# Attention's first group takes its rows by token halves, later stages' semaphores are credited in the first stage, and the output is stored in parts

## The chip, the cores and the metric

One Trainium2 chip, one of its cores. Five engines work side by side, each with an instruction stream of its own: TensorE (PE, with its weight loads shown as PEld), VectorE (DVE), ScalarE (ACT), GpSimd (POOL) and SyncE (SP), which here only issues transfers. They wait for each other through semaphores. The metric is the time of one execution on the device in microseconds; lower is better.

## The reference

Six blocks follow each other on x of 2 sequences x 1024 tokens x 256 channels, each behind a layer norm and added to x:

```
x = x + 0.5 * moe(norm(x))          # 16 experts, top 2, 256 -> 512 -> 256, silu
x = x + attention(norm(x))          # 16 heads of 16; scores of later keys are 0, not left out
x = x + 0.5 * moe(norm(x))
x = x + 0.5 * lora_ffn(norm(x))     # base linear + 8 low-rank experts, top 2
x = x + latent_attention(norm(x))   # 16 heads, rotary part, low-rank keys and queries
x = x + 0.5 * lora_ffn(norm(x))
```

## The kernel before

The kernel is written engine by engine. A stage is a `Block` in which each engine has its own program, and at the end of a block all engines meet in a barrier. x stays on the chip in the tile `X` (128 partitions x 16 token tiles x 256). The stages are `moe` (twice, with a short `load_stage` ahead of the first), `att`, `lora` 0, `mla`, `lora` 1 and a `store_stage`. Order within a stage is the order in which the code is written.

**Semaphores.** Nearly every semaphore of the kernel is counted from 1 (`Sem.base` is 1), and SP adds that 1 at the start of the stage in which the semaphore first occurs (`credit`, L113 to L117). The engines of a stage wait for the last one credited, as in `act.wait_ge(s_x.handle, s_x.at(0))`, before they do anything. Each credit is one instruction of SP on L116.

**Norms.** `norm_sd_act` (L131) waits for the means and variances `MV`, then takes the square root on ScalarE. ScalarE needs a function table for that (ACT_TABLE_LOAD). The moe, mla and second lora stages use it; attention and the first lora stage take four tiles at a time (`part_sd_act`, L143).

**Sums of the experts.** After a moe stage the two expert outputs of each token lie in DRAM (`rows_out`). The next stage loads them in four groups of four tiles (`ExpertSums.load`, tiles `Y1` and `Y2`, 512 KB a transfer) and DVE adds them to x two tiles at a time (`ExpertSums.add`, L219 to L234). `Y2` holds eight tiles, so groups 2 and 3 wait until groups 0 and 1 are added.

**Attention.** Heads are worked off in eight groups G of four. For each, `projections` makes 512 columns (a token half) of queries and keys, ACT and DVE split them into a high part `SH` and a low part `SL`, and SP places their rows in `QT` and `KT` by 12 transfers of 128 KB (L765) after both halves are made. `rough_scores` then makes score pieces of 128 to 512 keys, of which DVE takes the maxima (L1171, L1173); the first 16 pieces or so (`NPC0`) belong to the first 512 tokens, and need only keys of that half. `QT` and `KT` are first filled by ACT (L1099, L1100), for both buffers of the ring. In the front of the stage (before the loop over G) DVE adds the sums (`summed(0)` to `summed(3)`), normalizes tiles 0 to 7, makes the low parts and then runs `maxima(0, ...)`. PE transposes tiles 0 to 7, projects the two halves of group 0, multiplies the values of tiles 0 to 7 (`values`, L857) and then starts `rough_scores`.

**Lora.** For 16 tiles, PE transposes the rows (L1343), makes `mids` (L1335), then `base` (L1353) for tiles 0 to 3, into PSUM banks 4 to 7. While DVE works out the routing of tiles 8 to 15 PE waits; then, tile by tile, PE turns the gated mids (L1359), adds their product (L1390) to the base in its bank, DVE updates X (`updated`, L1509), and PE makes the base three tiles ahead as soon as the bank is free. The first lora stage also prepares weights for mla (`queries_into_keys`, `values_into_output`), which use banks 0 to 3 and are copied out by ACT.

**Store.** `store_stage` is a block of its own with one transfer of 2 MB (L2291).

## Time and profile before

| | |
|---|---|
| median of 3 runs | 2308.17 us (2306.41 to 2308.9) |
| time of the profiled execution | 2314.1 us |
| its span in the trace | 2312.4 us |
| PE busy | 2027.0 us (88%) |
| DVE busy | 1306.3 us (56%) |
| ACT busy | 787.8 us (34%) |
| POOL busy | 872.7 us (38%) |
| mean granted clock of PE | 0.928 |

The span is that of the trace, from the first to the last record. Roughly, moe 0 runs from 0 to 285 us, attention to 749, moe 1 to 1020, lora 0 to 1112, mla to 2253, lora 1 to 2304, and the store to the end. An engine's share of the whole says little about the places where the stages meet, since there most engines are idle together.

### The profile page before, as it was taken

To read this page: it belongs to the slowest core of one execution; us is meant where nothing else is said; L and a number is where in the kernel's file an instruction comes from. 1 tells how busy PE (TensorE), PEld (TensorE's weight loads), DVE (VectorE), ACT (ScalarE), POOL (GpSimd) and SP (SyncE) were. 2 spreads that over 40 slices of the span, in tenths; PEclk is the share of its full clock that TensorE was granted. 3 is DMA by queue.
4 is the path that set the end of the run, shared out by engine and by line. 5 is a ranking of instruction groups with operands and counts; after the bars stand their busy time and mean duration, and the time that the engine had idled before them with its cause. 6 is when DMAs were issued, how large, how long until landed. Compare 5 with 4: busy or idle time off the path is not lost. (4 is left out here: it accounts for less than half of the span.)

```text
span 2312.4 us, 29499 instructions
## 1 busy us (share of the span) xinstructions
PE 2027.0 (88%) x8740; PEld 1262.9 (55%) x8741; DVE 1306.3 (56%) x2992; ACT 787.8 (34%) x1297; POOL 872.7 (38%) x690
## 2 busy tenths in 40 slices
PE   5899859898988799965679999999899999999986
PEld 5566535455544666644545555555565555555455
DVE  6322265777785722236456667666656666666525
ACT  1122244555554122223214333334413333333312
POOL 0344301231112044431025555565325555555622
PEclk9999958999999599987679999999999999999998
DMA  9121242232220711232132211222022222222001
GB/s 370 46 63 61 53 118 28 28 44 39 28 28 7 332 55 64 60 103 105 43 70 55 52 46 42 54 54 55 18 65 55 55 50 55 54 54 51 9 2 47
DMA packets 59656, 151.40 MB, mean 65 GB/s; under 512 B 12768, under 2 KB 18096, under 8 KB 57264
## 3 DMA queue, kind: packets, MB, share of 16 engines
q1 hardware_dynamic: 49008, 120.43, 20.1%
q0 software_dynamic: 9408, 25.70, 3.8%
q10 hardware_dynamic: 1152, 4.19, 0.4%
q8 instruction: 43, 0.70, 0.1%
q14 instruction: 45, 0.37, 0.1%
HBM read 69.47 MB, written 18.87 MB: 38 GB/s over the span
## 5 line engine op out<-in xcount | busy, mean ns | idle before, releaser
L1723 POOL TENSOR_TENSOR mla_PS<-mla_PS,mla_PT 128x1024 f32<-128x1024 f32 x192 | 457.8, 2384 | 227.9 <-ACT mla_PT L2002 225.3
L2145 DVE TENSOR_REDUCE mla_MXP<-PS 128x1 f32<-128x512 f32 x512 | 343.4, 689 | 245.7 <-PE PS L1802 241.2
L2002 ACT ACTIVATE mla_PT<-PS 128x1024 f32<-128x1024 f32 x256 | 262.3, 1025 | 406.5 <-PE PS L1821 404.0
L1830 PE MATMUL PS<-mla_PT,mla_CN 128*64 128x512 f32 x1024 | 276.0, 618 | 0.1
L486 DVE COPY moe_HT<-PS 128x512 f32<-128x512 f32 x96 | 66.4, 692 | 320.0 <-PE PS L603 313.9
L1802 PE MATMUL PS<-mla_KH,mla_QH 113*128 113x512 f32 x512 | 216.7, 459 | 32.5 <-DMA mla_KL<-mla_SL 21.3
L618 POOL DMA_INDIRECT moe_XS<-rows_in,moe_GI x100 | 97.4, 974 | 317.1 <-PE PS L586 178.5
L1821 PE MATMUL PS<-mla_QH,mla_KH 113*128 113x512 f32 x512 | 211.9, 414 | 1.0 <-ACT mla_QH L1989 1.0
L1821 PE MATMUL PS<-mla_QL,mla_KH 113*128 113x512 f32 x512 | 202.8, 396 | 0.0
L1821 PE MATMUL PS<-mla_QH,mla_KL 113*128 113x512 f32 x512 | 201.6, 394 | 0.0
L1802 PEld LDWEIGHTS PS<-mla_KH,mla_QH 113*128 113x128 f32 x512 | 90.9, 193 | 194.5 <-DVE mla_MXP L2145 123.5
L1072 ACT ACTIVATE att_PT<-PS 128x1024 f32<-128x1024 f32 (+1 forms) x192 | 152.0, 811 | 94.4 <-PE PS L912 92.9
L597 PE MATMUL PS<-W,moe_ST 128*128 x384 | 177.6, 606 | 2.7 <-DVE moe_ST L481 2.7
L1723 POOL TENSOR_TENSOR mla_PS<-mla_PT 128x1024 f32<-128x1024 f32 x32 | 76.3, 2383 | 264.6 <-ACT mla_PT L2002 264.6
L611 PE MATMUL PS<-W,moe_HT 128*128 x768 | 173.7, 379 | 0.0
L891 PE MATMUL PS<-att_KT,att_QT 128*128 128x512 f32 (+3 forms) x384 | 146.1, 426 | 27.5 <-DVE att_MX L1173 10.1
L1171 DVE CUSTOM_DVE_ANT_0 PS<-PS,att_SEEN 128x128 f32<-128x128 f32 (+3 forms) x256 | 122.8, 508 | 55.6 <-PE PS L891 53.2
L611 PEld LDWEIGHTS PS<-W,moe_HT 128*128 128x128 f32 x768 | 142.3, 190 | 17.3
L791 POOL TENSOR_SCALAR_AFFINE_SELECT att_PT<-att_PT 128x256 f32<-128x256 f32 x128 | 52.0, 407 | 252.9 <-ACT att_PT L1072 252.8
L2157 DVE RECIPROCAL PS<-PS 128x128 f32<-128x128 f32 x128 | 108.7, 918 | 59.9 <-PE PS L1837 59.9
L1821 PEld LDWEIGHTS PS<-mla_QH,mla_KH 113*128 113x128 f32 x512 | 97.1, 190 | 80.6 <-issue 34.3
L891 PEld LDWEIGHTS PS<-att_KT,att_QT 128*128 128x128 f32 x384 | 75.6, 212 | 105.6 <-DVE att_MX L1173 38.5
(291 smaller groups left out, 3243.8 us busy)
## 6 DMA issues: line engine op xcount, KB each, us to landing
W<-in_W_dram SPq DMA_DIRECT2D x16, 2048.0 KB, 27.6
sums_Y<-rows_out SPq DMA_DIRECT2D x16, 512.0 KB, 4.9
mla_QH<-mla_SH SPq DMA_DIRECT2D x64, 128.0 KB, 2.4
mla_KH<-mla_SH SPq DMA_DIRECT2D x64, 128.0 KB, 2.4
mla_QL<-mla_SL SPq DMA_DIRECT2D x64, 128.0 KB, 2.4
mla_KL<-mla_SL SPq DMA_DIRECT2D x64, 128.0 KB, 2.4
mla_KH<-mla_SH SPq DMA_DIRECT2D x64, 96.0 KB, 2.4
mla_KL<-mla_SL SPq DMA_DIRECT2D x64, 96.0 KB, 2.4
```

What stands on the lines that cost most here:

```text
L597: ins = pe.matmul(bank(2 + u)[:, :], ST[:, u, k, :], g.W1[:, experts[u], k, :], start=(k == 0), stop=(k == KD - 1))
L611: ins = pe.matmul(bank(6 + u)[:, 0:D], HT[:, u, k, :], W2[:, experts[u], k, :], start=(k == 0), stop=(k == KF - 1))
L891: ins = pe.matmul(out[:, m, :], QT[:, H % 2, h, i * P:(i + 1) * P], KT[:, H % 2, h // 2, k0:k0 + w], start=(m == 0), stop=(m == len(hs) - 1))
L1072: act.activation(PT[:, kk % 2, 2 * pair:2 * pair + 2, c0:HB], st_banks(s)[:, :, c0:HB], ACT.Exp, scale=SEQ ** -0.5).then_inc(s_p.handle, 1)
L1171: ins = dve.tensor_tensor_reduce(part, part, seen, 1.0, LEAST, ALU.mult, ALU.max, MX[:, q, c, h, t:t + 1])
L1723: pool.tensor_tensor(PS[:, :], PT[:, slot(0), :] if k == 1 else PS[:, :], PT[:, slot(k), :], ALU.add).then_inc(s_ps.handle, 1)
L1802: pe.matmul(bank(piece_bank(n))[:, :], QH[USED, buf, h, tile * P:(tile + 1) * P], KH[USED, buf, h, c * HB:(c + 1) * HB], start=True, stop= ...
L1821: ins = pe.matmul(bank(st_bank(s, h))[:, :], kk[USED, buf, h, ks], qq[USED, buf, h, qs], start=(n == 0), stop=(n == 2))
L1830: ins = pe.matmul(bank(6)[h * DKVL:(h + 1) * DKVL, :], CN[:, b, k, 0:DKVL], PT[:, slot(k), h * HB:(h + 1) * HB], start=(k == 0), stop=(k = ...
L2002: act.activation(PT[:, slot(k), :], banks(st_bank(s, 0), 2)[:, :], ACT.Exp, scale=MLA_SCALE).then_inc(s_p.handle, 1)
L2145: dve.tensor_reduce(MXP[:, n // NPC, c, h, t:t + 1], bank(piece_bank(n))[:, :], AX_X, ALU.max).then_inc(s_mx.handle, 1)
L2157: dve.reciprocal(bank(A)[:, cols], bank(A)[:, cols]).then_inc(s_rc.handle, 1)
```

## The change

Seven edits, in the order of the program. (1) The square root's table is loaded ahead of the wait in `norm_sd_act`, in attention and in the first lora stage. (2) The first moe stage's SP program credits, after its own semaphores, all those of the later stages (`LATER`, a tuple of 100 or so names). (3) Group 0 of the sums is loaded in two halves of two tiles with a semaphore each; in attention `Y2` now lies in the tile `PT`, holds 16 tiles, and groups 2 and 3 no longer wait. (4) Attention's group 0 places its rows by token halves, in 24 transfers of 64 KB, the first 12 with a semaphore of their own; `rough_scores` of the first block waits for those alone. DVE makes the first low part ahead of `summed(2)`, PE multiplies the values of tiles 0 and 1 between the halves, and ACT's fills of the second buffer stand behind the row copies. (5) The lora stages keep six bases in PSUM in place of four. (6) PE's wait for the lora weights stands ahead of the first `mids` and no longer ahead of the first transposes. (7) The second lora stage stores the output in four parts of 512 KB, each after four tiles are updated, and `store_stage` is gone.

```diff
 def norm_sd_act(act, g, s_mv, s_sd):
+    g.nc.scalar.preload_act_table(ACT.Sqrt)
     act.wait_ge(s_mv.handle, s_mv.at(NT))
...
+            if n == 0:
+                for half in range(2):
+                    tiles = slice(2 * half, 2 * half + 2)
+                    sp.dma_start(self.Y1[:, tiles, :], rows(0)[:, tiles, :]).then_inc(self.s_in[half].handle, 16)
+                    sp.dma_start(self.Y2[:, tiles, :], rows(1)[:, tiles, :]).then_inc(self.s_in[half].handle, 16)
+            else:
+                sp.dma_start(self.Y1[:, tiles, :], rows(0)[:, tiles, :]).then_inc(self.s_in[n + 1].handle, 16)
+                sp.dma_start(self.Y2[:, ring, :], rows(1)[:, tiles, :]).then_inc(self.s_in[n + 1].handle, 16)
...
                 g.credit(sp)
                 if rep:
                     expert_weights(g, dram, rep)(sp)
+                else:
+                    for name in LATER:
+                        g.sem(name)
+                    g.credit(sp)
...
-        expert = g.sums.buffers(ctx)
+        expert = g.sums.buffers(ctx, PT[:, :, :, :].rearrange("p u h (n d) -> p (u h n) d", d=D))
...
-                sp.wait_ge(s_afill.handle, s_afill.at(4))
                 for G in range(NG):
+                    if G < 2:
+                        sp.wait_ge(s_afill.handle, s_afill.at(2 * (G + 1)))
...
+                    for half in range(2 if G == 0 else 1):
+                        tok = slice(half * HB, (half + 1) * HB) if G == 0 else slice(0, SEQ)
+                        s_placed = s_first if G == 0 and half == 0 else s_rows
...
+                            sp.wait_ge(s_made.handle, s_made.at(half + 1 if G == 0 else 2 * (G + 1)))
...
-                        if n == 0:
+                        if H == 0 and n == 0:
+                            pe.wait_ge(s_first.handle, s_first.at(NROW))
+                        elif n == (NPC0 if H == 0 else 0):
                             pe.wait_ge(s_rows.handle, s_rows.at(NROW * (H + 1)))
...
                     projections(0, half, bank(4 + half))
-                for t in range(TB):
-                    if t >= 2:
-                        pe.wait_ge(s_vc.handle, s_vc.at(t - 1))
+                    if half == 0:
+                        for t in range(2):
+                            values(t, bank(2 + t))
+                for t in range(2, TB):
+                    pe.wait_ge(s_vc.handle, s_vc.at(t - 1))
                     values(t, bank(2 + t % 2))
...
+                low(0, 0, bank(4))
                 summed(2)
-                low(0, 0, bank(4))
                 low(0, 1, bank(5))
...
+    BASE = (4, 5, 6, 7, 2, 3)
+    NB = len(BASE)
...
+                if out is not None:
+                    s_out = g.sem("x_stored")
+                    rows = out.rearrange("b (t p) d -> p (b t) d", p=P)
+                    for n in range(NB4):
+                        tiles = slice(n * NT // NB4, (n + 1) * NT // NB4)
+                        sp.wait_ge(s_x.handle, s_x.at((n + 1) * NT // NB4))
+                        sp.dma_start(rows[:, tiles, :], g.X[:, tiles, :]).then_inc(s_out.handle, 16)
+                    sp.wait_ge(s_out.handle, s_out.at(16 * NB4))
...
-                pe.wait_ge(s_w.handle, s_w.at(64))
-
                 def mids_of(t):
+                    if t == 0:
+                        pe.wait_ge(s_w.handle, s_w.at(64))
...
+                pe.wait_ge(s_xtc.handle, s_xtc.at(NT))
                 if ahead:
-                    pe.wait_ge(s_xtc.handle, s_xtc.at(NT))
                     queries_into_keys()
                     values_into_output(0)
                     values_into_output(1)
-                    pe.wait_ge(ahead.s_abc.handle, ahead.s_abc.at(2))
+                    pe.wait_ge(ahead.s_abc.handle, ahead.s_abc.at(6))
+                else:
+                    pe.wait_ge(s_mid.handle, s_mid.at(NT))
+                for t in range(NR, NB):
+                    base(t)
...
-            lora_stage(nc, g, dram, 1)
-        store_stage(nc, g, out)
+            lora_stage(nc, g, dram, 1, out=out)
```

How the instructions stand, at the places of which the prediction speaks. First ScalarE at the start of attention, before (`att_QT`, `att_KT`: the fills; `att_XT`: transposed rows; `att_SH`: high parts; `att_VV`: values; SD: the root):

```order
L1099 ACTIVATE att_QT<-C 128x4096 [waits att_x_updated]
L1100 ACTIVATE att_KT<-C 128x2048
L1099 ACTIVATE att_QT<-C 128x4096
L1100 ACTIVATE att_KT<-C 128x2048
L147 ACT_TABLE_LOAD
L147 ACTIVATE SD<-MV,C 128x4 [waits norm_stats]
L1035 COPY att_XT<-PS 128x2x128 [waits att_xnT_in_psum] x4
L1049 CAST att_SH<-PS 128x512 [waits att_qk_in_psum]
L147 ACTIVATE SD<-MV,C 128x4 [waits norm_stats]
```

And of the change:

```order
L1147 ACT_TABLE_LOAD [waits att_x_updated]
L1142 ACTIVATE att_QT<-C 128x4096
L1145 ACTIVATE att_KT<-C 128x2048
L166 ACTIVATE SD<-MV,C 128x4 [waits norm_stats]
L1076 COPY att_XT<-PS 128x2x128 [waits att_xnT_in_psum] x4
L1142 ACTIVATE att_QT<-C 128x4096
L1092 CAST att_SH<-PS 128x512 [waits att_qk_in_psum]
L166 ACTIVATE SD<-MV,C 128x4 [waits norm_stats]
L1080 COPY att_VV<-PS 128x16x16 [waits att_values_in_psum] x2
```

The table and one pair of fills stand ahead of the first root; the second pair has moved behind the first copies, and two copies of values stand behind the second root.

Second SP at the same place, from the weights on, before (`sums_Y`: expert sums; 12 transfers of L765, of which the first two stand here):

```order
L753 DMA att_Wo<-in_Wo_dram 128x512
L216 DMA sums_Y<-rows_out 128x1024 [waits moe_second_added,moe_expert_out_stored]
L217 DMA sums_Y<-rows_out 128x1024
L216 DMA sums_Y<-rows_out 128x1024 [waits moe_second_added]
L217 DMA sums_Y<-rows_out 128x1024
L765 DMA att_QT<-att_SH 16x2x1024 [waits att_high_parts,att_filled_by_act]
L765 DMA att_KT<-att_SH 16x2x1024
```

And of the change:

```order
L786 DMA att_Wo<-in_Wo_dram 128x512
L244 DMA sums_Y<-rows_out 128x1024 [waits moe_expert_out_stored]
L245 DMA att_PT<-rows_out 128x1024
L244 DMA sums_Y<-rows_out 128x1024
L245 DMA att_PT<-rows_out 128x1024
L802 DMA att_QT<-att_SH 16x2x512 [waits att_high_parts,att_filled_by_act]
L802 DMA att_KT<-att_SH 16x2x512
```

The groups behind the weights have lost their wait for DVE, and the row transfers carry 512 tokens each (12 of them for each half).

Third TensorE in the second lora stage, behind the first bases, before:

```order
L1353 MATMUL PS<-lora_Wbase,lora_XT 128x256 x8
L1359 MATMUL PS<-C,lora_GM 128x128 [waits lora_gated] x2
L1390 MATMUL PS<-lora_B,lora_MT 128x256 [waits lora_midsT_copied]
L1359 MATMUL PS<-C,lora_GM 128x128 [waits lora_midsT_copied,lora_gated]
L1390 MATMUL PS<-lora_B,lora_MT 128x256 [waits lora_midsT_copied]
L1353 MATMUL PS<-lora_Wbase,lora_XT 128x256 [waits lora_x_updated]
```

And of the change:

```order
L1416 MATMUL PS<-lora_Wbase,lora_XT 128x256 x8
L1416 MATMUL PS<-lora_Wbase,lora_XT 128x256 [waits lora_mids_copied,lora_xnT_copied]
L1416 MATMUL PS<-lora_Wbase,lora_XT 128x256 x3
L1422 MATMUL PS<-C,lora_GM 128x128 [waits lora_gated] x2
L1457 MATMUL PS<-lora_B,lora_MT 128x256 [waits lora_midsT_copied]
L1422 MATMUL PS<-C,lora_GM 128x128 [waits lora_midsT_copied,lora_gated]
L1457 MATMUL PS<-lora_B,lora_MT 128x256 [waits lora_midsT_copied]
L1416 MATMUL PS<-lora_Wbase,lora_XT 128x256 [waits lora_x_updated]
```

Two bases (four rows) have moved ahead of the first turn of gated mids; the loop that follows makes 10 bases where it made 12.

## Rows read from the trace of the kernel before

**Rows 1.** Page, parts 1 and 2: busy time, and PE's granted clock in tenths by 40 slices.

```profile
PE 2027.0 (88%) x8740; PEld 1262.9 (55%) x8741; DVE 1306.3 (56%) x2992; ACT 787.8 (34%) x1297; POOL 872.7 (38%) x690
...
PEclk9999958999999599987679999999999999999998
```

**Rows 2.** Instructions of L116 in attention, lora 0 and mla: ns, first and last start.

```profile
L116 SPq EVENT_SEMAPHORE  x37: 17/17/17, 285.4 to 288.0; - x37
...
L116 SPq EVENT_SEMAPHORE  x26: 17/17/17, 1019.8 to 1021.3; - x26
...
L116 SPq EVENT_SEMAPHORE  x38: 17/17/17, 1111.9 to 1114.0; - x38
```

**Rows 3.** Timeline of attention's front: start, duration, operation [idle before <-releaser].

```profile
293.43 0.88 DVE L225 SCALAR_TENSOR_TENSOR X<-sums_Y,GH,X 128x256 f32<-128x256 f32 x2 [4.54 <-DMA sums_Y<-rows_out]
...
298.74 1.28 ACT L147 ACT_TABLE_LOAD   x1
...
301.13 1.09 PE L851 MATMUL PS<-C,att_XNS 128*128 128x128 f32 x4 [19.16 <-DVE att_XNS L159]
...
307.76 0.58 ACT L1049 CAST att_SH<-PS 128x512 fp32r<-128x512 f32 x1 [3.87 <-PE PS L876]
...
310.80 0.88 DVE L225 SCALAR_TENSOR_TENSOR X<-sums_Y,GH,X 128x256 f32<-128x256 f32 x2
...
315.55 7.07 PE L857 MATMUL PS<-att_Wv,att_XT 128*128 128x256 f32 x32
...
323.25 0.43 DVE L153 RECIPROCAL RS<-SD 128x4 f32<-128x4 f32 x2 [1.30 <-ACT SD L147]
...
331.94 0.30 DVE L1171 CUSTOM_DVE_ANT_0 PS<-PS,att_SEEN 128x128 f32<-128x128 f32 x1 [8.25 <-PE PS L891]
...
341.20 0.17 DVE L1183 TENSOR_SCALAR att_MB<-att_MX 128x16 fp32r<-128x16 f32 x1
```

**Rows 4.** Line L765, 310 to 332 us: one form of its four, and issue to landing.

```profile
L765 SPq DMA_DIRECT2D att_QT<-att_SL x2: 591/592/592, 322.2 to 323.5; - x2
...
DMA to landing us min/median/max: 3.5/5.7/7.4
```

**Rows 5.** Timeline: last weight load of attention, and line L753 from issue to landing.

```profile
291.08 0.43 SPq L753 DMA_DIRECT2D att_Wo<-in_Wo_dram  x1
...
DMA to landing us min/median/max: 8.0/8.0/8.0
```

**Rows 6.** Timeline: the root's table in moe 0 (first two) and mla.

```profile
15.33 1.28 ACT L134 ACT_TABLE_LOAD   x1 [15.33 <-DVE MV L128]
16.62 0.31 ACT L134 ACTIVATE SD<-MV,C 128x16 f32<-128x16 f32 x1
...
1115.35 1.28 ACT L134 ACT_TABLE_LOAD   x1 [5.76 <-DVE MV L128]
```

**Rows 7.** Timeline: start of lora 0, first addition.

```profile
1026.72 0.88 DVE L225 SCALAR_TENSOR_TENSOR X<-sums_Y,GH,X 128x256 f32<-128x256 f32 x2 [12.81 <-DMA sums_Y<-rows_out]
```

**Rows 8.** Timeline: start of lora 1.

```profile
2258.22 1.12 PE L1343 MATMUL PS<-C,lora_XN 128*128 128x128 f32 x4 [6.29 <-DMA lora_biases<-in_biases_dram]
...
2259.37 1.27 PE L1335 MATMUL PS<-lora_Wlora,lora_XT 128*128 128x136 f32 x4
```

**Rows 9.** Timeline: updates of X in the last stage (tiles 11, 13, then 14 and 15).

```profile
2299.73 0.42 DVE L1509 SCALAR_TENSOR_TENSOR X<-PS,X 128x256 f32<-128x256 f32 x1 [0.78 <-PE PS L1390]
...
2302.54 0.42 DVE L1509 SCALAR_TENSOR_TENSOR X<-PS,X 128x256 f32<-128x256 f32 x1 [0.98 <-PE PS L1390]
...
2303.16 0.97 DVE L1509 SCALAR_TENSOR_TENSOR X<-PS,X 128x256 f32<-128x256 f32 x2 [0.20 <-PE PS L1390]
```

**Rows 10.** The store: timeline, transfers (KB each, us to landing), and L216, a 512 KB load.

```profile
2304.49 0.40 SPq L2291 DMA_DIRECT2D out_dram<-X  x1
...
out_dram<-X SPq DMA_DIRECT2D x1, 2048.0 KB, 7.5
...
DMA to landing us min/median/max: 3.9/4.1/6.3
```

More of the change, by code:

```diff
@@ L197, in __init__, with buffers @@
         self.s_yd = S("expert_out_stored", 16 * NTILE, pool_dma=True)
-        self.s_in = [S(f"sums_loaded{n}", 32) for n in range(self.NG)]
+        self.s_in = [S(f"sums_loaded{n}", 32) for n in range(self.NG + 1)]
         self.s_first, self.s_second, self.s_stats = S("first_added", NT), S("second_added", NT), S("row_stats", NT)
         self.rep = rep
-    def buffers(self, ctx):
-        self.Y1, self.Y2 = (self.g.sb(ctx, f"sums{self.rep}_{n}", [P, tiles, D]) for n, tiles in (("Y1", NT), ("Y2", NT // 2)))
+    def buffers(self, ctx, second=None):
+        name = f"sums{self.rep}_Y"
+        self.Y1 = self.g.sb(ctx, name + "1", [P, NT, D])
+        self.Y2 = self.g.sb(ctx, name + "2", [P, NT // 2, D]) if second is None else second
+        self.y2_tiles = NT // 2 if second is None else NT
         return self
@@ L1256, in _, with lora_stage @@
                     updated(TB + i, bank(i % 2))
-def lora_stage(nc, g, dram, rep, ahead=None):
+def lora_stage(nc, g, dram, rep, ahead=None, out=None):
     S = lambda name, each: g.sem("lora_" + name, each, rep)
@@ L1389, in _ @@
                     pe.wait_ge(s_mtc.handle, s_mtc.at(t + 1))
-                    pe.matmul(bank(4 + t % NR)[:, 0:D], MT[:, t % NR, :], BL[:, :], start=False, stop=True).then_inc(s_lo.handle, 1)
-                    if t and t + NR - 1 < NT:
-                        base(t + NR - 1)
+                    pe.matmul(bank(BASE[t % NB])[:, 0:D], MT[:, t % NR, :], BL[:, :], start=False, stop=True).then_inc(s_lo.handle, 1)
+                    if t and t + NB - 1 < NT:
+                        base(t + NB - 1)
             @block.scalar
             def _(act):
-                if not sums:
+                if sums:
+                    nc.scalar.preload_act_table(ACT.Sqrt)
+                else:
                     norm_sd_act(act, g, s_mv, s_sd)
@@ L2282, in _ @@
                         updated(b, i)
-def store_stage(nc, g, out):
-    s_out = g.sem("x_moved")
-    with nc.Block() as block:
-        @block.sync
-        def _(sp):
-            g.credit(sp)
-            sp.dma_start(out.rearrange("b (t p) d -> p (b t) d", p=P), g.X[:, :, :]).then_inc(s_out.handle, 16)
-            sp.wait_ge(s_out.handle, s_out.at(16))
 def macaron_program(nc, dram, out, stages="mamlLl"):
```

64 lines of the change are left out of this document (44 added, 20 removed).

## The prediction

> **What bounds the kernel now.** I read the page first: TensorE is busy 88% of the span [rows 1], so where it is dense only less work for it would help, and this change takes none away. What the change touches are the seams between stages. There the question is which wait ends last, and I read that from the timeline around each seam, with idle time and its releaser. Four kinds of waste show.
>
> First, SP's credits. In attention 37 of them run from 285.4 to 288.0 us, in lora 0 26 from 1019.8 to 1021.3, in mla 38 from 1111.9 to 1114.0 [rows 2]; no engine does work of the stage before the last one. That is 2.6, 1.5 and 2.1 us, or 0.07 us each. Second, in moe 0 ScalarE's table load starts only when the norm's inputs are there (15.33), and the root follows at 16.62 [rows 6]: 1.28 us on a chain on which everything else of the stage waits. It is the same in moe 1 and mla. Third, attention's front. DVE gets the first sums at 293.43; it starts the maxima at 331.94 after 8.25 us of idling, because the rows of the whole first group had to land; before that it was never long idle, from 310.80 to the last reciprocal at 323.25 to 323.68 [rows 3]. So behind the row transfers DVE is next in line. Fourth, the end: the last update ends at 2303.16 + 0.97 = 2304.13, and the store of 2 MB is issued at 2304.49 and lands 7.5 us later [rows 9, 10].
>
> **The change part by part.**
>
> *Root's table.* Loaded ahead of the wait, it runs in idle time (ScalarE sits idle 15.33 us before it in moe 0 and 5.76 in mla). That gives 1.3 us each in moe 0, moe 1 and mla: 3.9. If the cover were gone it would cost the 1.28 it costs now. The root starts 0.01 us after the load [rows 6], so I count the load alone. The Trainium skill (ScalarE: Activation LUTs, What ACT_TABLE_LOAD costs) gives about 2.66 us for a switch of tables, 1283 ns for the load and about 1380 for a drain. The trace agrees on the load and shows no drain here; by the page the three places would give 8.0 in place of 3.9.
>
> *Credits.* They move to SP in moe 0, behind the semaphores on which that stage's start depends, and SP has nothing else to do there. About 103 x 0.07 = 7 us of SP, hidden behind 270 us of moe 0. One semaphore more stands ahead (the halves of group 0): +0.07. Gain 2.6 in attention (counted below), 1.5 in lora 0, 2.1 in mla.
>
> *First sums by halves.* A 512 KB transfer takes about 4.1 us to land [rows 10], the first addition waits for two of them, and I take the second to add some 1.2 us (2 MB of the store land in 7.5 us, against 4.1 for a quarter of it: 3.4 / 3 = 1.1). With half the bytes it starts about 1.2 us earlier, in attention and in lora 0, where the first addition at 1026.72 is waited for after 12.81 us of idling [rows 7]. Between nothing and 2 us. What follows in lora 0 is DVE's own work, so it carries over. Groups 2 and 3 without waits in attention: DVE never waited for them, nothing.
>
> *Attention's front.* The first addition comes at 293.43 - 2.6 - 1.2 = 289.6. Four tiles are done 5 us later, 294.6, and ScalarE has then been free since 292.2 (285.4, the table 1.28, a pair of fills 5.5); before, its two pairs of fills and the table load ended at 300.02 [rows 3]. That would be 5.4 earlier, but PE also waits for the last weight, which landed at 291.08 + 8.0 = 299.1 [rows 5]. It has the same bytes ahead of it and starts 2.6 earlier: 296.5. So PE's first transposes move from 301.13 to 296.5, by 4.6. The high part of half 0 moves from 307.76 to 303.1 likewise. Then PE does the values of tiles 0 and 1: 7.07 us for eight tiles [rows 3] is 0.9 for one at the high clock (1.8 at the low one, at which this place ran), 1.8 to 3.5 us where it had idled 1.6. So the second half of the transposes comes up to 1.8 later than it could, and DVE begins low part and sums at 310.80 - 4.6 + 1.8 = 308.0, against 306.2 without that. DVE's chain of low parts, sums and reciprocals took 323.68 - 310.80 = 12.9 us, and it had to wait 1.3 us in it for ScalarE, which stood in values copies. Some 0.9 of that goes, since two copies are out of the way: it ends at 320.0. Are the rows there? SP issues half 0 from 303.7: eight high transfers at 0.6 us [rows 4], four low ones behind DVE's low part at 308.7, issued by 311.2, landed by 314.7 (3.5) or 318.6 (7.4). PE's values end at about 318. So DVE no longer waits and the maxima start at 320.0 in place of 331.94: 11.9 us. With the high clock at TensorE in this stretch (it projects and multiplies values without a break for 7 us) the 1.8 falls away: 13.7. I take 12.5, between the two and nearer the low clock, at which the rows ran.
>
> The second half's rows must be there when the first block's maxima end. These took 341.20 - 331.94 = 9.3 us, so 329.3. High part 1 at about 313; SP issues 12 transfers at 0.6 us each, to 320.5, and they land 3.5 to 7.4 later, 324 to 328. That is covered, by 1 to 5 us; every us beyond would count fully. ScalarE's second pair of fills is behind the copies and hidden in the projections; if it is not, it costs up to 3.6.
>
> *Six banks.* In the loop of both lora stages a tile with a base takes 1.41 us (2299.73 to 2302.54 is two), and without one about 0.6 (2302.54 to 2303.16) [rows 9]. Two bases move to where PE waits for the routing: 2 x 0.8 = 1.6 us in each stage. In lora 0 they stand behind ScalarE's copies of the absorbed weights, still in DVE's routing time.
>
> *Lora 1's start.* PE's first transposes at 2258.22 were released by the weights' transfer; they now go ahead, and the first mids take their place, which came at 2259.37 [rows 8]: 1.15. The root's table is hidden here by the same transfer, so I count nothing for it.
>
> *Store.* The last part is 512 KB and is issued some 0.1 us after the last update, without a barrier. Loads of that size took 3.9 to 6.3 us, median 4.1 [rows 10]. Against 2304.49 + 7.5 - 2304.13 = 7.9 it ends 3.9 earlier, or 1.5 by the slow end. The earlier parts have 1.4 us a tile to run in and are gone.
>
> **Sum.** Moe 0 1.2, attention 12.5, moe 1 1.3, lora 0 1.5 + 1.2 + 1.6 = 4.3, mla 2.1 + 1.3 = 3.4, lora 1 1.1 + 1.6 + 3.9 = 6.6: 29.3 us. The profiled execution took 2314.1, so 2284.8; the median of the runs is 5.9 lower, 2308.2, so **2279 us**, 1.3% less.
>
> **The rivals.**
>
> *A: attention's front gives little.* The row transfers stay last: 24 that each occupied their queue as a whole one did. The 12 were issued 0.6 us apart, and issue to landing grew from 3.5 to 7.4 us [rows 4], so the queue took 0.6 + 3.9 / 12 = 0.93 us for each. Halves at the same price land by 303.7 + 12 x 0.93 + 2.9 = 317.8 for half 0, and about 329 for half 1 (behind half 0 in the queue). That just meets the 329.3. Together with a high part that comes late by 3.6 (the fills) the front gives 7 in place of 12.5: 2284. The Trainium skill (DMA: Bandwidth & Descriptors, Bandwidth) speaks against this edit: it asks for transfers of 1 MiB or more and calls those under 64 KB descriptor-dominated, with 0.95 us for 64 KB. By the page a half takes 11.4 us of queue; half 1 would land at about 326, and the time would not change.
>
> *B: TensorE's clock helps.* In the profile it was at 0.5 to 0.9 in two places, attention's front and the start of moe 1 [rows 1]. The change fills idle time of PE between the halves and in both lora stages; if the clock stays at 2.4 GHz through the rough scores, the pieces and later values run faster by up to 5 us: 2273.
>
> *C: the page's price for tables.* If the root's table really held up 2.66 us each, the gain is 4 more: 2275. Against it speaks the 0.01 us between load and root.
>
> *D: no change.* The seams could be bound by something else that comes at a fixed time, a transfer above all. For lora 1's start this is so and counted; elsewhere the releasers are the credits, DVE and ScalarE. Then within 0.2% of before: 2306.
>
> *E: slower.* The granted clock of TensorE. The main loops of attention and mla are PE's, and mostly at full clock [rows 1]. A us at half clock there costs about half a us. If moving the stages made the clock low for 60 us more than before, the 29 are gone, and beyond that it is slower; at 80 us the time is 2319. The slices show some 4 to 6 of 40 with any low share outside the fronts, so this would be several times what there is. Nothing in the change makes PE idle in those loops.
>
> **How the numbers follow.** Forecast (22 to 36 us gained) 0.82, A 0.09, B in its full size (over 36) 0.03, C 0.02, D 0.01, E 0.03. The bounds of the unknown costs are: attention 11 to 17 (low or high clock), store 1.5 to 4.4, halves of sums 0 to 4 in both, banks 0 to 3.5. Not all fall on one side; 2269 to 2289 holds the forecast's body and part of A, and leaves 2 in 10 out. Within 0.2% (4.6 us), about what a measurement of this kernel can tell from no change: 0.02. Faster by more: 0.95; slower by more: 0.03.
>
> **What the new profile would show.** Attention's first DVE addition about 4 us after the last engine of moe 0; ScalarE's root ahead of any second fill; maxima starting right behind the reciprocals, with no idle time released by PE's rough scores; that idle time would prove A. Credits of L116 nearly all in the first 30 us. Lora's updates 0.6 us apart for the last five tiles. The last store landing about 4 us after the last update. The prediction is wrong if DVE idles again for rows, if PE waits for the weights beyond 297, or if PEclk is lower in mla.

## The result and the profile after

The changed kernel takes 2278.89 us (median of four runs, 2278.29 to 2280.76), the kernel before 2308.18 (2306.41 to 2308.9): a ratio of 0.9876, with a 95% interval of 0.9858 to 0.9893. The forecast was 2279. The traced execution took 2279.0 us with a span of 2277.3. Its page, parts 1 and 2, answers to [rows 1]:

```profile
PE 2015.8 (89%) x8740; PEld 1256.3 (55%) x8741; DVE 1306.4 (57%) x2992; ACT 788.2 (35%) x1297; POOL 872.5 (38%) x690
...
PEclk9999969999999599987679999999999999999999
```

TensorE does the same 8740 matmuls, its share of a shorter span is higher, and of the clock's digits the 5 and 8 of attention's front have become 6 and 9 and the last 8 a 9.

Attention's front, timeline of the changed kernel; it answers to [rows 3]:

```profile
287.30 0.88 DVE L254 SCALAR_TENSOR_TENSOR X<-sums_Y,GH,X 128x256 f32<-128x256 f32 x2 [3.00 <-DMA att_PT<-rows_out]
...
296.41 1.09 PE L888 MATMUL PS<-C,att_XNS 128*128 128x128 f32 x4 [16.48 <-DMA att_Wo<-in_Wo_dram]
...
302.58 1.89 PE L894 MATMUL PS<-att_Wv,att_XT 128*128 128x256 f32 x8
302.78 0.59 ACT L1092 CAST att_SH<-PS 128x512 fp32r<-128x512 f32 x1
...
304.37 0.73 PE L888 MATMUL PS<-C,att_XNS 128*128 128x128 f32 x4
...
306.58 1.98 PE L913 MATMUL PS<-att_XT,att_Wqk 128*128 128x512 f32 x4 [0.46 <-ACT att_XT L1076]
...
313.39 0.75 PE L930 MATMUL PS<-att_KT,att_QT 128*128 128x128 f32 x4
...
317.24 0.30 DVE L1224 CUSTOM_DVE_ANT_0 PS<-PS,att_SEEN 128x128 f32<-128x128 f32 x1
...
326.51 0.18 DVE L1236 TENSOR_SCALAR att_MB<-att_MX 128x16 fp32r<-128x16 f32 x1
```

TensorE's first transposes are released by the last weight at 296.41 (296.5 was forecast). The maxima start at 317.24 with no bracket behind them: the 8.25 us of idling are gone, and DVE goes on where its last reciprocal ends. The first rough scores (L930) start at 313.39, so the rows of the first half were there 3.8 us before DVE was. The row transfers, all 24, by line (one form of four) and their landing; this answers to [rows 4]:

```profile
L802 SPq DMA_DIRECT2D att_QT<-att_SL x4: 583/592/593, 309.3 to 318.5; - x4
...
DMA to landing us min/median/max: 2.2/2.2/2.6
```

The credits, and the last two updates, against [rows 2] and [rows 9]:

```profile
L134 SPq EVENT_SEMAPHORE  x154: 17/17/17, 0.8 to 20.4; - x154
```

```profile
2271.19 0.42 DVE L1578 SCALAR_TENSOR_TENSOR X<-PS,X 128x256 f32<-128x256 f32 x1 [0.79 <-PE PS L1457]
...
2271.81 0.97 DVE L1578 SCALAR_TENSOR_TENSOR X<-PS,X 128x256 f32<-128x256 f32 x2
2272.97 0.97 DVE L1578 SCALAR_TENSOR_TENSOR X<-PS,X 128x256 f32<-128x256 f32 x2 [0.20 <-PE PS L1457]
```

All credits lie in the first 20.4 us, and the last five updates are 0.6 us apart. The span ends 4.33 us after 2272.97; before it was 2312.4 - 2303.16 = 9.24.

**Where the time went, stage by stage.** I traced both kernels a second time. The table gives the length of each stretch in both traces of each, from starts read in the timelines; its ends are the last scatter of moe 0 on POOL, attention's first maxima, attention's last row statistics, the last copy of moe 1 on DVE, the last statistics of lora 0, mla's reciprocal, mla's last statistics, the start of the last two updates, and the end of the span. The gain is the difference of the two means.

| stretch | before (2 traces) | changed (2 traces) | gain | forecast |
|---|---|---|---|---|
| moe 0 | 282.66, 282.90 | 280.62, 281.50 | 1.7 | 1.2 |
| attention to the first maxima | 49.28, 49.41 | 36.62, 37.58 | 12.2 | 12.5 |
| rest of attention | 416.43, 414.69 | 414.61, 414.35 | 1.1 | 0 |
| moe 1 | 264.79, 263.95 | 264.04, 264.10 | 0.3 | 1.3 |
| lora 0 | 97.72, 99.74 | 96.24, 96.60 | 2.3 | 4.3 |
| mla to its reciprocal | 6.18, 6.19 | 2.72, 2.72 | 3.5 | 3.4 |
| rest of mla | 1135.37, 1129.35 | 1131.18, 1131.19 | 1.2 | 0 |
| lora 1 to the last updates | 50.73, 50.50 | 46.94, 46.78 | 3.8 | 2.7 |
| store | 9.24, 9.27 | 4.33, 4.28 | 4.9 | 3.9 |
| sum | 2312.4, 2306.0 | 2277.3, 2279.1 | 31.0 | 29.3 |

The fronts are sharper than the whole: two traces of one kernel agree within 0.3 us in most of them. Three places vary more. In the three traces taken later in which attention's front is that of the changed kernel (the runs with late roots, four banks and the store apart), it took 37.06, 36.50 and 36.33 us, so with the two of the table it spreads over 1.25 us. Lora 0 of the kernel before took 97.72 and 99.74 us, and 97.79 in a third trace (the run with the halves alone), so its usual gain is nearer 1.3 than 2.3. And the main loops add 1.1 and 1.2 to the gain, which is within what they vary.

### The profile page after: what moved, and what is told of

It is laid out like the page before. It is cut to its first block and busy times, and to the rows that moved or that the text cites. A ratio compares the mean times of both kernels' runs of the same rounds, so it can differ in the third digit from the quotient of the medians.

```text
span 2277.3 us, 29510 instructions
## 1 busy us (share of the span) xinstructions
PE 2015.8 (89%) x8740; PEld 1256.3 (55%) x8741; DVE 1306.4 (57%) x2992; ACT 788.2 (35%) x1297; POOL 872.5 (38%) x690
## 3 DMA queue, kind: packets, MB, share of 16 engines
q10 hardware_dynamic: 1152, 4.19, 0.5%
## 5 line engine op out<-in xcount | busy, mean ns | idle before, releaser
L930 PE MATMUL PS<-att_KT,att_QT 128*128 128x512 f32 (+3 forms) x384 | 145.7, 424 | 24.2 <-DVE att_MX L1226 10.1
L930 PEld LDWEIGHTS PS<-att_KT,att_QT 128*128 128x128 f32 x384 | 74.7, 210 | 102.1 <-DVE att_MX L1226 38.5
```

Of the source, the lines that this page charges most:

```text
L930: ins = pe.matmul(out[:, m, :], QT[:, H % 2, h, i * P:(i + 1) * P], KT[:, H % 2, h // 2, k0:k0 + w], start=(m == 0), stop=(m == len(hs) - 1))
```

## The experiments

The kernels ran in three groups of four, each group on one chip beside the kernel before. Medians of the same kernel vary by 1 to 2.5 us and single runs by 5 and more, so I read each edit's price in its own stretch of the trace and hold the whole time beside it. The changed kernel itself ran in the first group alone (2277.62 us), and "more than the changed kernel" means this one in all groups. The kernel before took 2309.69, 2309.75 and 2310.69 us beside the three groups, so such a difference in the third group (values behind, halves alone, store apart, waits cut finer) may be 1 us too high. Not undone by themselves were the early tables of attention and lora 0, the sixteen tiles of `Y2`, the first low part ahead of the third sums, the moved fills, and edit (6).

**A second trace of each kernel.** Nothing edited.

> The kernel before, unchanged, for a second trace of it. The profiled execution of before took 2314.1 us, 5.9 more than the median. In it the latent attention lasted 1139.1 us from its first mean (1114.08) to that of the next stage (2253.16); in the changed kernel 1133.6 (1093.17 to 2226.77), of which only 1.3 is the root's table. Theory 1 (chance): this execution was a slow one, and a new trace shows some 1135 there and a span of 2305 to 2308. Theory 2 (the change did it): a new trace shows 1139 again, and the change shortened a loop in which it moves nothing.

2308.58 us, ratio 0.9998 (0.9988 to 1.0008); the traced execution had a span of 2306.0. The rest of mla took 1129.35 us and not 1135.37: theory 1. Two windows of mla, 1569 to 1669 and 1869 to 1969, first of the first trace of before, then of the second; the last three columns are granted clock, DMA share and GB/s:

```profile
1569.00:1669.00 100.00, 91.31 (x386) 52.31 (x386) 65.86 (x107) 42.14 (x91) 50.38 (x23) 0.95 0.14 32
...
1869.00:1969.00 100.00, 96.19 (x378) 52.70 (x377) 65.36 (x98) 38.38 (x49) 56.16 (x27) 0.98 0.24 57
```

```profile
1569.00:1669.00 100.00, 91.17 (x393) 52.02 (x389) 67.74 (x110) 41.58 (x91) 49.14 (x22) 0.97 0.15 34
...
1869.00:1969.00 100.00, 96.51 (x388) 53.20 (x384) 67.61 (x102) 37.40 (x48) 58.67 (x28) 1.00 0.22 53
```

The same program, and 7 and 10 matmuls fewer in 100 us where the granted clock is 0.02 lower. So 5.9 us by which the first trace stood above the median lay in mla's loop.

> The changed kernel, unchanged, on the same chip as the next runs, as the measure for them. Time 2278 to 2281 us. Its trace shows how far a stage's length varies from one execution to the next: I expect under 0.5 us in the stages ahead of the latent attention, and up to 4 in the latter.

2277.62 us, ratio 0.9859 (0.9843 to 0.9876). The stages' lengths are in the table. Two stretches ahead of mla differed by more than 0.5, moe 0 by 0.9 and attention's front by 1.0. In the latter TensorE's first transposes waited for the weights till 298.46, 10.6 us behind the first addition and not 9.1.

**Rows whole again.** Core of the edit against the changed kernel:

```diff
-                    for half in range(2 if G == 0 else 1):
-                        tok = slice(half * HB, (half + 1) * HB) if G == 0 else slice(0, SEQ)
-                        s_placed = s_first if G == 0 and half == 0 else s_rows
+                    for half in range(1):
+                        tok = slice(0, SEQ)
+                        s_placed = s_rows
```

> The changed kernel, with attention's first group placing its rows as before: 12 transfers of 128 KB after both halves are made, and the rough scores waiting for all of them. Forecast's theory (the rows were last, and the halves took them off the path): in before the last row was there 14.75 us after the high part of half 1 (316.33 to 331.08); here that part is ready at 309.2, so the scores start at 324.0 and the maxima at 324.8 in place of 317.24: 7.6 us longer, 2286.5. Rival A (the halves gave nothing, the gain came from the earlier start of everything): the maxima start at 317 to 318 and the time stays within 1 us of the changed kernel. Third theory (the long landing in before came from other traffic at that moment, loads of sums): the transfers land 2.2 us after issue, as the halves do, the last at 318.9, maxima at 319.8, 2.5 us longer, 2281.4.

2285.18 us, ratio 0.9893 (0.9877 to 0.991), 7.6 more than the changed kernel on this chip. Timeline of DVE, and the landing of its 12 transfers:

```profile
317.45 0.18 DVE L172 RECIPROCAL RS<-SD 128x4 f32<-128x4 f32 x1 [0.37 <-ACT SD L166]
325.28 0.30 DVE L1220 CUSTOM_DVE_ANT_0 PS<-PS,att_SEEN 128x128 f32<-128x128 f32 x1 [7.66 <-PE PS L928]
```

```profile
DMA to landing us min/median/max: 3.5/5.7/7.4
```

DVE idles 7.66 us again. From the end of moe 0 to the maxima it is 44.47 us against 37.1 (mean of the changed kernel's two traces): 7.4. Theory 1; rival A in the form tested here, by which this edit should have changed nothing, has fallen. The third theory has fallen too, since the landing is as long as in [rows 4] at another time and beside other loads.

**Halves, but late.**

```diff
-                            sp.wait_ge(s_made.handle, s_made.at(half + 1 if G == 0 else 2 * (G + 1)))
+                            sp.wait_ge(s_made.handle, s_made.at(2 * (G + 1)))
```

> The changed kernel with its 24 transfers of 64 KB for attention's first group, but each of them issued only after both halves are made; the first 12 still have their own semaphore. It separates the size of a transfer's rows (2 KB in place of 4 KB) from the earlier start. In the trace 1.57 MB of row transfers took 12.2 us of the queues as 12 wholes (67.6% of 18 us) and 6.8 us as 24 halves (37.9% of 18). Theory 1 (size of rows matters): from 309.2 the first 12 halves are issued 0.63 us apart and land 2.2 us behind, the twelfth at 309.3 + 12 x 0.63 + 1.7 = 318.6 (the low parts, made at 311.6, are in time), so the maxima start at 319.5, 2.2 us later than in the changed kernel: 2281. Theory 2 (only the earlier start matters, a half costs the queue as much as a whole): the twelfth lands as late as the twelfth whole, 324, and the maxima start at 324.8: 2286.5.

2281.72 us (2274.48 to 2283.98), ratio 0.9873 (0.9851 to 0.9896). In the trace the maxima wait little:

```profile
318.67 0.30 DVE L1224 CUSTOM_DVE_ANT_0 PS<-PS,att_SEEN 128x128 f32<-128x128 f32 x1 [2.47 <-PE PS L930]
```

2.47 us of idling, and 38.61 us from moe 0's end to the maxima, 1.5 more than the changed kernel and 5.9 less than with wholes issued at the same moment. So most of what the halves gave comes with the smaller transfers, and only the rest with their earlier start; theory 2 has fallen. Part 3 of two windows of 18 us, first 12 wholes (the kernel before, 314 to 332), then 24 halves (the changed kernel, 303 to 321):

```profile
q1 hardware_dynamic: 576, 1.57, 67.6%
```

```profile
q1 hardware_dynamic: 1152, 1.57, 37.9%
```

The same 1.57 MB takes 12.2 us of the queues in the one and 6.8 in the other. That it is not the 128 KB of a transfer shows in mla of the changed kernel, where transfers of 128 KB, each 64 rows of 2 KB, are issued 0.64 us apart as well (here one kind of four):

```profile
mla_QH<-mla_SH SPq DMA_DIRECT2D x64, 128.0 KB, 2.4
```

They land after 2.4 us. There each transfer also writes 64 partitions and not 16, so the length of a row and the bytes that a partition takes are not told apart.

The 5.9 us are not yet the price of long rows. The awaited 12 halves also carry half the bytes. Even at half of a whole's 12.2 / 12 = 1.02 us a half would take 0.51 us of the queues, less than the 0.63 between two issues, and would not queue. Fewer bytes ahead of the first consumer, or the cheaper byte, would each have ended the queueing; how the 5.9 us divide between them no run shows.

**The halves alone, in the kernel before.** The loop of SP, TensorE's wait and ScalarE's wait of edit (4), nothing else of it.

> The kernel before with one part of the change alone: attention's first group places its rows by halves (24 transfers of 64 KB, the first 12 awaited by the first block's rough scores). Nothing else is moved: SP still waits for all of ScalarE's fills, DVE makes its first low part behind the third sums. In the trace of before the high part of half 0 was made at 308.3 and the low one at 316.4, so the last of the first 12 is issued at 318.9 and, at 2.2 us, lands at 321.1; DVE's reciprocals end at 323.7. Theory 1 (rows were all that was late): the maxima start at 323.9 in place of 331.94, 8.0 us earlier, and the time is 2300.5. Theory 2 (the gain needs the other moves too, the earlier low part above all): half of it or less, 2304 to 2308.

2298.85 us (2296.05 to 2300.76), ratio 0.9953 (0.9937 to 0.997). The maxima start 40.19 us after moe 0's end, 9.2 less than before (8.0 was expected), with no wait for rows. The wait for them was 8.25; TensorE's clock rose at 306.1 in this trace and at 315.3 in that of before, and how much of the rest goes with that is not shown. The whole time is 11.8 us less than the kernel before beside it. Theory 1: this part needs none of the others.

**Values behind the second projection.**

```diff
-                    if half == 0:
-                        for t in range(2):
-                            values(t, bank(2 + t))
-                for t in range(2, TB):
-                    pe.wait_ge(s_vc.handle, s_vc.at(t - 1))
+                for t in range(TB):
+                    if t >= 2:
+                        pe.wait_ge(s_vc.handle, s_vc.at(t - 1))
```

ScalarE's two copies of these values move behind the second high part with them (not shown).

> The changed kernel, with the values of tiles 0 and 1 behind the second projection again, where they stood before, and not between the halves. It tests rival B, the granted clock. In the changed kernel TensorE worked without a break from 296.4 to 304 and its clock was at 2.4 GHz from 302.7 on; in before it idled 1.6 us between the halves and had 1.2 GHz until 315.7. Theory 1 (the filled gap brought the clock up 13 us sooner): here the second half's transposes and projection run at 1.2 GHz (1.09 us for four transposes and 3.5 us for the projection, in place of 0.73 and 1.98) and the maxima start 1 to 2 us later behind the first addition than the 29.9 and 31.2 us of the two traces of the changed kernel. Theory 2 (the clock rises there whatever stands between the halves): transposes 0.73 and projection 1.98, and the maxima start 0 to 0.5 us earlier.

2280.91 us (2280.11 to 2285.74), ratio 0.9872 (0.9855 to 0.9888). Timeline of TensorE, and of DVE ahead of the maxima:

```profile
304.27 0.73 PE L888 MATMUL PS<-C,att_XNS 128*128 128x128 f32 x4 [1.76 <-DVE att_XNS L178]
305.28 1.09 PE L888 MATMUL PS<-C,att_XNS 128*128 128x128 f32 x4 [0.28 <-DVE att_XNS L178]
306.83 3.78 PE L913 MATMUL PS<-att_XT,att_Wqk 128*128 128x512 f32 x4 [0.46 <-ACT att_XT L1074]
...
318.91 0.43 DVE L172 RECIPROCAL RS<-SD 128x4 f32<-128x4 f32 x2 [2.05 <-ACT SD L166]
```

Neither theory as written: the clock did rise (four transposes in 0.73 us), but behind TensorE's gap of 1.76 us it fell again, and the projection took 3.78 us where the changed kernel took 1.98. The granted clock was 1.0 from 302 to 305 and 0.5 from 305.3 to 310. The maxima start 32.6 us behind the first addition (29.9 and 31.2), and 39.05 behind moe 0's end: 2.0 more than the mean of two traces, 1.5 to 2.7 more than the five traces with the changed kernel's front. The 2 us come in at the end: DVE's third sums start as early as in the changed kernel (305.97 and 306.07), but its last reciprocals wait 2.05 us for ScalarE's roots, which stand behind the copies of the values, and TensorE starts these 2.0 us later (310.40 and 308.40). So the values between the halves, for which the forecast took up to 1.8 off, gave about 2, through the clock that rival B spoke of.

**The first sums whole.** Group 0 loaded by two transfers with one semaphore, as before.

> The changed kernel, with group 0 of the expert sums loaded as a whole again (two transfers of 512 KB, one semaphore for the pair), in attention and in the first lora stage. Forecast's theory: 1.2 us in each of the two stages, 2.4 in all, so 2280 us where the changed kernel takes 2277.6 on such a chip. Rival, from the trace of the changed kernel: there the second pair of additions waits (1.16 us in attention, 1.40 in lora 0), and in attention TensorE waits for the last weight till 296.4 whatever the additions do. Then the halves give 1.7 - 1.4 = 0.3 us in lora 0 and nothing in attention, and the time stays within 1 us. In the trace of lora 0 the third pair of additions decides: 1014.76 in the changed kernel is 18.9 us behind the last copy of moe 1 (995.89); Forecast's theory says 20.1, the rival 19.2.

2279.16 us (2276.55 to 2280.44), ratio 0.987 (0.9853 to 0.9886). The first pair of additions, and the second right behind it:

```profile
289.53 0.88 DVE L248 SCALAR_TENSOR_TENSOR X<-sums_Y,GH,X 128x256 f32<-128x256 f32 x2 [4.54 <-DMA att_PT<-rows_out]
...
292.00 0.85 DVE L248 SCALAR_TENSOR_TENSOR X<-sums_Y,GH,X 128x256 f32<-128x256 f32 x2
```

The first addition comes 8.2 us after moe 0's end (6.5 in the changed kernel), but the second pair waits no more, and the maxima start after 36.12 us, no later than the 36.62 and 37.58. Lora 0 lasts 96.44 against 96.24 and 96.60. The halves of the sums gave nothing: the rival. Its reason holds for the changed kernel alone, though. With the sums whole TensorE's first transposes started 14.33 us behind moe 0's end (15.79 in the changed kernel) and were released by DVE's rows and not by the weight, which SP issued 0.85 us sooner without the two extra transfers ahead of it.

**The root's table late.** The preload in `norm_sd_act` is taken out.

> The changed kernel, with the square root's table loaded behind the norm's wait again in moe 0, moe 1, mla and the second lora stage (attention and the first lora stage keep the new place). Forecast's theory: 1.3 us each in moe 0, moe 1 and mla, nothing in lora 1: 3.9 us, so 2281.5. Rival, from two traces of each kernel: moe 1 from its first maxima of the router to its last copy takes 254.4 and 253.6 us before, and 255.2 and 255.3 in the changed kernel, so what the root gave there (1.3) was taken back by the granted clock, whose stretch at 1.2 GHz ends no earlier for it. Then moe 1 ends no later here than in the changed kernel, its stretch from router maxima to last copy takes 254.0 to 254.4 again, and the whole is 2.6 us longer, 2280.2. The page's price of 2.66 us a switch would make it 8.0 us longer, 2285.6.

2285.04 us (2279.66 to 2285.86), ratio 0.99 (0.9883 to 0.9916), 7.4 above the changed kernel. The trace, of the run of 2279.66, shows less: the root in moe 0 starts at 16.60, 1.3 later; moe 1 takes 264.83 us (0.8 more), mla's front 4.02 (1.3 more), and lora 1 45.58 (1.3 less, for which I have no reason). The load still stands alone ahead of the root, here in moe 1:

```profile
735.67 1.28 ACT L152 ACT_TABLE_LOAD   x1 [3.80 <-DVE MV L146]
736.96 0.31 ACT L152 ACTIVATE SD<-MV,C 128x16 f32<-128x16 f32 x1
```

That is 2.1 us in the trace. The other three runs, at 2284 to 2286, had a granted clock of 0.935 to 0.936 and the traced one 0.938, so the clock goes with part of the other 5 us, but a run of the changed kernel at 0.934 took 2280.76; in which stretch the rest lies no trace shows. The Trainium skill (ScalarE: Activation LUTs, What ACT_TABLE_LOAD costs) has 2.66 us for a switch of tables; the estimate of 8.0 us from it fits the median better than the forecast's 3.9 or the rival's 2.6. The trace speaks against its drain of 1380 ns: the root starts 0.01 to 0.02 us behind the load in all four places, and a drain would have lengthened each of the three stretches by 2.7.

**Credits in their stages.** The loop over `LATER` is taken out.

> The changed kernel, with each stage crediting its own semaphores at its start again (only the one for the stored output is credited at the start of the second lora stage, ahead of which there was a block of its own). Forecast's theory: 2.6 us in attention, 1.5 in lora 0 and 2.1 in mla, 6.2 in all, 2283.8. In the trace attention's first addition, lora 0's first addition and mla's first mean each come that much later after the last work of the stage before. Rival (part of it is hidden, since transfers and weights follow the credits on SP's queue, and the granted clock gives some of lora 0's back): 4 us or less, under 2281.6.

2290.3 us (2286.71 to 2293.14), ratio 0.9916 (0.9899 to 0.9933), 12.7 more than the changed kernel. In the trace attention takes 40.35 us to its maxima (3.2 more), lora 0 97.18 (0.8 more, though only 0.2 more than the longest of the other runs, 96.97; 1.5 at its first addition, of which half is lost on the way) and mla's front 5.34 (2.6 more): 6.6. The wait as it stands in mla:

```profile
1100.90 1.17 DVE L146 BATCH_NORM_AGGREGATE MV<-ST 128x2 f32<-128x6 f32 x16 [2.89 <-SPq L134]
```

The forecast's 6.2 is right for the sum of the stretches, within what attention's front varies. Of the other 6 us most lies in the rest of mla, 1137.70 us against 1131.19, where nothing was edited; this run had a clock of 0.931 and was the longest of the four. At a clock of 0.938 this kernel took 2286.71 us, and the changed one 2279.0 and 2280.93: 5.8 to 7.7, which agrees with the stretches.

**Four banks.** `BASE = (4, 5, 6, 7)`.

> The changed kernel, with four PSUM banks for the bases of both lora stages in place of six. Forecast's theory: two bases go back into the loop, 0.8 us each in each stage: 3.2 us, 2280.8. From the traces: the second lora stage took 19.96 us from its first to its last update before and 16.63 in the changed kernel, 3.3 us less; the first took 1.1 to 1.7 less from its second routing to the end. By these it is 4.4 to 5.0 us longer, 2282 to 2282.6: the two bases come off the loop's end (1.6) and another 1.7 off its start, where TensorE at the low clock made a base for each of the first tiles before it could go on.

2283.84 us (2282.96 to 2284.98), ratio 0.9894 (0.9878 to 0.9911), 6.2 more. Lora 0 97.84 us (1.4 more), lora 1 49.99 (3.1 more): 4.5, the rival's price.

**The store apart.** A block of its own with one transfer of 2 MB.

> The changed kernel, with the output stored in a block of its own again, by one transfer of 2 MB. Forecast's theory: 3.9 us, the difference between the landing of 2 MB and that of a 512 KB load (4.1), so 2281.6. From the traces, where the span ended 9.24 and 9.27 us behind the start of the last two updates before and 4.33 and 4.28 in the changed kernel: 4.95 us, 2282.6.

2281.99 us (2279.23 to 2286.12), ratio 0.9884 (0.9867 to 0.99), 4.4 more (3.4 against the kernel before of its group). From the last updates to the end it is 9.13 us against 4.3: 4.8.

**Three waits cut finer.** An attempt to beat the changed kernel. Not shown are the lines of the lora stages, where the routing weights get a semaphore of their own, and the bases and DVE's biases wait for the rest:

```diff
-                pe.wait_ge(s_w.handle, s_w.at(48))
...
+                    if half == 0:
+                        pe.wait_ge(s_w.handle, s_w.at(48))
                     projections(0, half, bank(4 + half))
...
-                    for n in range(NB4):
-                        tiles = slice(n * NT // NB4, (n + 1) * NT // NB4)
-                        sp.wait_ge(s_x.handle, s_x.at((n + 1) * NT // NB4))
+                    ends = (0, 4, 8, 12, 14, 16)
+                    for first, last in zip(ends, ends[1:]):
+                        tiles = slice(first, last)
+                        sp.wait_ge(s_x.handle, s_x.at(last))
```

> The changed kernel with three waits cut finer: attention's TensorE waits for its weights ahead of the first projections and no longer ahead of the first transposes; in the lora stages the routing weights have a semaphore of their own, so that the first mids no longer wait for the biases; and the last part of the store is two tiles (the parts are 4, 4, 4, 2 and 2). Theory (these three waits are what is last at their places): in attention TensorE's first transposes started 9.1 and 10.6 us behind the first addition, though the rows were ready after 6.9 (287.30 to 294.2), so the maxima come 2.2 to 3.5 us earlier; in lora 1 the first mids waited 1.95 us for the biases: 1.9 us; the store ended 4.3 us after the start of the last updates, and a part of half the size gives 0.5: 5 us in all, 2273. Rival (something else is next in each place: the weights are needed by the projections 2.8 us later anyway, the low clock takes lora 1's part back): 1 to 2 us, 2276.

2280.1 us (2274.8 to 2282.86), ratio 0.9862 (0.9843 to 0.988): not to be told from the changed kernel. Only the store gained (3.50, 0.8 less). Attention's maxima start after 36.33 us, which the run with the store apart had too without this edit, and lora 1 took 46.40, within the 46.32 to 47.07 of other runs without it, though its first mids came 1.75 us behind the reciprocal and not 3.4. The rest of mla took 3.6 more than in the changed kernel's traces. It is the rival's case: in attention TensorE's first transposes are now released by DVE's rows, 7.79 us behind the first addition, and what follows takes the gain back.

## Why the prediction was right

The median, 2278.89 us, is the forecast 2279, and the sum of terms, 29.3 us, is the difference of the medians. That they meet so closely is in part luck: lora 0 gave 2 us less than forecast, lora 1 and the store 1 us more each, and 2.3 of the table's 31.0 us come from the main loops, which the change does not touch; the other stretches gave 28.7. The seams were right as the places where the time lay, and so was what was last at most of them.

- **Attention, 12.5 forecast, 12.2 measured.** Weights till 296.5 (296.41), the high part at 303.1 (302.78) and no wait for rows held. Two steps were wrong and cancelled in part. The halves of the first sums were to give 1.2 and gave nothing, since the second pair then waits (1.16 us, from its start at 291.00) and TensorE waits for the weights anyway, which the two extra transfers put off. And the values between the halves were to cost up to 1.8, at the low clock; the clock went to 2.4 GHz there, DVE's low part and third sums came 2 us sooner than forecast (305.5 and 306.1 against 308.0), and they gave about 2. By their own runs credits give 3.2, rows 7.4, values 2.0 and sums nothing, 12.6 together. Of the rows I saw the cause only in part: I counted them as started earlier, and that is 1.5 of it. The rest is that the queue no longer backs up: wholes took it for 1.02 us each (12.2 / 12), more than the 0.63 between issues, and halves take 0.28 (6.8 / 24).
- **Rival A** put a half at 0.93 us, the rate of a whole; the trace has 0.28. The Trainium skill warns of small transfers (DMA: Bandwidth & Descriptors, Bandwidth: 0.95 us for 64 KB). That figure was measured from HBM to SBUF over 128 partitions and with GpSimd issuing, and it does not carry over to these copies within the chip issued by SP: here 24 transfers of 64 KB were issued 0.63 us apart and landed 2.2 to 2.6 us later, none queueing behind another.
- **Rival B** was priced at up to 5 us and gave 2. Its reading of [rows 1] left out a third place with a low clock, the digits 8767 from the end of moe 1 through lora 0 to the start of mla, and there the forecast of lora 0 failed.
- **Credits, 6.2 forecast.** 6.6 in their stretches, so right; undoing them cost 12.7, and the rest lay mostly in mla's loop at a lower granted clock, whose cause is open.
- **Root's table, 3.9 forecast.** 1.3, 0.8 and 1.3 in the traces of moe 0, moe 1 and mla, so mla and moe 0 are right. In moe 1 part of the gain was given back: from the router's first maxima to the last copy it is 255.2 us with the early root and 254.4 and 253.6 before. The stage became 0.8 shorter and not 1.3; the 0.3 of the table comes from one trace of before (263.95), where three others with the late root took 264.79 to 264.83, against 264.01 to 264.10 in nine of ten with the early one. What took the rest back I haven't shown. The whole time of the run without it leaves 5 us open, as told.
- **Lora 0, 4.3 forecast, 2.3 measured.** Credits 0.8 in place of 1.5, sums nothing in place of 1.2, banks 1.4 (1.6). Against two of the three traces of before it is 1.3, little more than the banks alone. The step that failed is "what follows is DVE's own work, so it carries over": the first addition came 3.2 us earlier behind moe 1's last copy (10.3 against 13.5), but the last of the mids on TensorE only 0.4 earlier (57.5 against 57.9 us, first traces).
- **Lora 1, 2.7 forecast, 3.8 measured.** The banks gave 3.1 and not 1.6: I counted the two bases at the loop's end and missed its start: there the second and third gap between updates shrank from 2.02 and 2.72 us to 1.65 and 1.41, and with four banks they were 1.99 and 2.76 again. In before TensorE's clock was at 1.2 GHz during the 2.72. The first mids came about as much earlier as forecast (6.94 us behind mla's last statistics before, 5.88 now), but 0.7 is all that is left for it beside the banks.
- **Store, 3.9 forecast, 4.9 measured.** The last part lands some 3.4 us behind the end of the last update; for it I had taken the 4.1 of a load [rows 10]. By the prediction's own terms the gain was 7.9 - 0.1 - 4.1 = 3.7 and not 3.9. And before, the span ended 8.2 us behind the last update and not 7.9.
- **The base.** Summing against the traced execution and taking off its 5.9 us was right: the second trace put these in mla's loop. Compared with the first trace alone the gain would be 35.1, and 6 of it no effect of the change.

Of the signs named, one failed in one trace of two: TensorE waited for the weights till 298.46, beyond 297. The maxima moved by 1 us for it.

## What to carry to other kernels

Where an engine idles for several transfers, look at the share of the queues that they take and not at their size alone: cutting them so that the first consumer needs half of them gave 7 to 9 us here, because the wholes took longer in the queue (1.02 us) than SP took to issue them (0.63) and the halves did not. A price belongs to a stretch and not to the whole: with runs that vary by 5 us, stretches that agree within 0.3 us told 1 us apart, but only after several traces had shown which of them agree so well. And ask what is next at each place: the halves of the sums, the credits of lora 0 and the three finer waits gave all or part of their gain to the wait behind them.

## What the runs showed of the hardware

- Rows of 4 KB and of 2 KB, placed from one on-chip tile into another, are not alike: 1.57 MB as 576 packets took the queues 12.2 us, as 1152 packets 6.8 (and 67.5% of 18 us again for the wholes of the kernel with that edit undone). Landing was 3.5 to 7.4 us in the one and 2.2 to 2.6 in the other. Transfers of 128 KB in rows of 2 KB, issued as closely in mla, landed after 2.4 us.
- TensorE's granted clock fell back to 1.2 GHz behind a gap of 1.76 us, just after it had risen: four transposes took 0.73 us and the next four 1.09. With two tiles' values in the place of the gap it stayed at 2.4 GHz.
- A kernel's executions differ by 5 to 8 us with their mean granted clock (with the credits in their stages 2286.71 us at 0.938 and 2293.14 at 0.931; with the three waits 2274.8 at 0.938 and 2282.86 at 0.935), and two traces of the kernel before, of 2314.1 and 2307.67 us, differ by 6.0 us in mla's loop, where both ran the same program.
